# Cross attention of a Perceiver block: folds two at a time between the halves of the Wo and context products, and ScalarE's exponentials last in most steps

## The reference, cut to what matters

```
x = x + xattn(layernorm(x), ctx)     # the stage that is changed
x = x + attn(layernorm(x))
x = x + ffn(layernorm(x))            # shared expert and 2 of 8 routed experts

def xattn(query, ctx):               # query 64 x 64 x 256, ctx 64 x 256 x 256
    q = query @ Wq + bq              # 16 heads of 64
    k = ctx @ Wk + bk;  v = ctx @ Wv + bv
    attn = softmax(q k^T / 8)
    out = (attn v) @ Wo + bo + query
    return layernorm(out) * gamma + beta
```

## Time and profile before

| what | value |
|---|---|
| time, median of 3 runs | 2296.89 us (2295.93 to 2297.06) |
| the profiled execution's own time | 2297.97 us |
| its span | 2296.2 us |
| TensorE busy | 2151.3 us, 94% of the span |
| VectorE, ScalarE, GpSimd busy | 1584.7, 1267.9 and 709.7 us |
| a group of the cross attention | 88.46 us (603.64 to 692.10) |
| cross attention | to about 1440 us of the span |

### The profile page before, as it was taken

The page is one execution under the profiler, slowest core; times in us unless marked ns, Lnnn a source line. Parts: engine busy times, 40 slices in busy tenths (PEclk is TensorE's granted clock), DMA queues, the critical chain, the costliest instruction groups (busy, mean ns, idle before and its releaser), DMA issues. The chain is left out here.

```text
span 2296.2 us, 48591 instructions
## 1 busy us (share of the span) xinstructions
PE 2151.3 (94%) x16836; PEld 1870.7 (81%) x16837; DVE 1584.7 (69%) x2992; ACT 1267.9 (55%) x3071; POOL 709.7 (31%) x677
## 2 busy tenths in 40 slices
PE   6999999999999999999999999788897996999997
PEld 6888888888888888888888888667775885888886
DVE  6767767767768667677677676578885755666665
ACT  5656555555556556555565555356664334555554
POOL 4001001001011010010010010367774274777775
PEclk9999999999999999999999999899997998999999
DMA  4001001000010010010010001252224221333332
GB/s 145 15 15 33 14 18 32 6 26 23 9 32 23 9 32 18 14 32 18 14 32 14 18 10 40 85 182 76 78 76 163 82 86 39 54 53 54 55 53 44
DMA packets 103215, 104.41 MB, mean 45 GB/s; under 512 B 14064, under 2 KB 92656, under 8 KB 103152
## 3 DMA queue, kind: packets, MB, share of 16 engines
q1 hardware_dynamic: 87280, 84.62, 11.7%
q0 software_dynamic: 15872, 18.95, 5.2%
HBM read 72.73 MB, written 30.81 MB: 45 GB/s over the span
## 5 line engine op out<-in xcount | busy, mean ns | idle before, releaser
L534 ACT ACTIVATE probs<-banks,nbias 128x256 f32<-128x256 f32 x512 | 235.6, 474 | 231.7 <-DVE nbias L664 231.3
L876 PE MATMUL banks<-ctxT_hi,qk_hi 128*128 128x256 f32 x1024 | 302.0, 295 | 0.0
L876 PE MATMUL banks<-ctxT_hi,qk_lo 128*128 128x256 f32 x1024 | 290.4, 284 | 0.0
L876 PE MATMUL banks<-ctxT_lo,qk_hi 128*128 128x256 f32 x1024 | 289.3, 282 | 0.0
L622 DVE TENSOR_TENSOR pT_lo<-banks,pT_hi 128x512 fp32r<-128x512 f32 x256 | 166.4, 685 | 165.2 <-ACT pT_hi L496 163.8
L496 ACT ACTIVATE qk_hi<-banks 128x512 fp32r<-128x512 f32 x256 | 139.7, 619 | 153.7 <-PE banks L919 150.7
L622 DVE TENSOR_TENSOR qk_lo<-banks,qk_hi 128x512 fp32r<-128x512 f32 x256 | 158.8, 682 | 86.7 <-ACT qk_hi L496 86.7
L876 PE MATMUL banks<-pT_hi,ctx_hi 128*128 128x512 f32 x512 | 208.0, 406 | 3.9 <-DVE pT_lo L622 2.9
L422 POOL TENSOR_TENSOR rstd<-mv,power 128x2 f32<-128x2 f32 x32 | 22.2, 693 | 603.1 <-DVE mv L705 603.1
L876 PE MATMUL banks<-pT_hi,ctx_lo 128*128 128x512 f32 x512 | 202.1, 395 | 0.0
L876 PE MATMUL banks<-pT_lo,ctx_hi 128*128 128x512 f32 x512 | 200.9, 392 | 0.0
(11 more groups left out here) (258 smaller groups left out, 5955.8 us busy)
## 6 DMA issues: line engine op xcount, KB each, us to landing
ctx_raw<-in_ctx_dram SPq DMA_DIRECT2D x64, 256.0 KB, 2.7
experts_w<-in_L_ffn_We_dram SPq DMA_DIRECT2D x24, 512.0 KB, 8.3
x_in<-in_x_dram SPq DMA_DIRECT2D x16, 256.0 KB, 2.9
x_again<-in_x_dram SPq DMA_DIRECT2D x16, 256.0 KB, 2.8
x_stream<-z SPq DMA_DIRECT2D x16, 256.0 KB, 2.2
s_x<-x_stream SPq DMA_DIRECT2D x32, 128.0 KB, 2.1
s_x_again<-x_stream SPq DMA_DIRECT2D x32, 128.0 KB, 2.1
x_normalised<-s_xl SPq DMA_DIRECT2D x32, 128.0 KB, 1.7
```

Source lines behind the costliest of these rows:

```text
L534: nc.scalar.activation(probs[:, s % 2, p, :], scores[:, s % 2, p // 2, (p % 2) * SK:(p % 2 + 1) * SK], ACT.Exp, bias=nbias[:, s % 2, p:p + ...
L876: last = nc.tensor.matmul(out, a, b, start=(n == 0), stop=(n == 3 * len(pairs) - 1))
```

## The change

Three edits, all of order; no instruction of arithmetic is added or removed.

1. Steps 3 and 7 (`b == 3`): before, two folds (`EARLY = 2`), both halves of pc, six folds. Now a loop of four turns has two folds at the end of each turn, and ahead of them at most one piece of other work. In step 7: folds 0 and 1; pc 0, folds 2 and 3; pc 1, folds 4 and 5; qbk, folds 6 and 7. In step 3: o 0, folds 0 and 1; o 1, folds 2 and 3; pc 0, folds 4 and 5; pc 1, folds 6 and 7. The ring's order, TensorE, ScalarE and VectorE follow alike.
2. VectorE in step 7: the remainders of folds 0 and 1 come ahead of `peaks`.
3. ScalarE: the exponentials of steps 0, 1, 4, 5 and 7 come at the end of the step, behind the read-out of pc and pT, where they were ahead of them. Those of steps 2, 3 and 6 keep their place, but in step 3 they now stand ahead of folds 0 and 1.

```
+def part_of_pc(half, i):
+    c = i - (1 if half else 2)
+    return c if 0 <= c < DC else None
...
 # TensorE; ScalarE, VectorE and ring_order have the same loop
-                if s == 3 and g.prev:
-                    do_o(g)
-                if b == 3 and (g.next if half else g.cur):
-                    do_fold(g, half, range(EARLY))
-                if (g.cur if s >= 2 else g.prev):
+                if b == 3:
+                    for i in range(HALF // 2):
+                        c = part_of_pc(half, i)
+                        if s == 3 and g.prev and i < TILES:
+                            do_o(g, i)
+                        if g.cur and c is not None:
+                            do_pc(g, s, [c])
+                        if s == 7 and g.next and i == 3:
+                            do_qbk(g)
+                        if (g.next if half else g.cur):
+                            do_fold(g, half, (2 * i, 2 * i + 1))
+                elif (g.cur if s >= 2 else g.prev):
                     do_pc(g, s)
-                if b == 3 and (g.next if half else g.cur):
-                    do_fold(g, half, range(EARLY, HALF))
-                if s == 7 and g.next:
-                    do_qbk(g)
...
 # ScalarE
-                if b == 3 and (g.next if half else g.cur):
-                    for h in range(EARLY):
-                        fold_upper(g, half, h)
-                if g.cur:
+                if g.cur and s in (2, 3, 6):
                     exps(g, s)
...
                 if (g.cur if s >= 1 else g.prev):
                     for k in range(KC):
                         pT_upper(g, s, k)
+                if g.cur and s not in (2, 3, 6):
+                    exps(g, s)
...
 # VectorE
                 if s == STEPS - 1 and g.next:
                     ctx_lower(g, b)
+                    for h in range(2):
+                        fold_lower(g, half, h)
                 if g.cur:
                     peaks(g, s)
...
+                if b == 3:
+                    for i in range(half, HALF // 2):
+                        if s == 3 and g.prev and i < TILES:
+                            bank, free = wait_filled(dve, g, ("o", i))
+                            nc.vector.tensor_tensor(z[:, i, :], bank[:, 0:D], resid[:, i, :], ALU.add).then_inc(free, 1)
+                        if s == 7 and g.next and i == 3:
+                            keep_qbk(g)
+                        if (g.next if half else g.cur):
+                            for h in (2 * i, 2 * i + 1):
+                                fold_lower(g, half, h)
```

## The result

Measured together with the kernel before, 6 runs each: 2242.07 us (2240.76 to 2244.75) against 2295.7 us (2291.99 to 2297.06), a ratio of 0.9769 with a 95% interval of 0.9757 to 0.9782. The kernel is 53.6 us faster; 42.7 were predicted against the same median. The profiled execution took 2244.75 us, its span is 2243.0.

The account below looks back on a forecast made before the run. TensorE, busy 94%, was taken as the bound. Savings of 2.92 us a group, 41 over 14 groups, 43 with groups 0 and 15, plus 2 for the clock, gave 2253 us; range 2244 to 2264, wider 2238 to 2280.

Parts of the forecast that it names:

- my own case: Whole kernel at 2244 to 2264 us, smaller terms off by a third, step 7 by 0.5 us; chance 0.60.
- more than I count: Rival: all of step 7's 2.89 us saved, no loss in step 5; 2234 us, or 2243 with half; chance 0.08.
- Step 7: Fold pairs spread between pc and qbk: 13.15 us in place of 15.05, 1.90 saved, bounds 0 and 2.89.
- Step 3: Both halves of o spread between pairs of folds: 17.5 us, 0.5 saved, bounds 0 and 0.6.
- Steps 1, 2 and 6: With exponentials last, pT and q are read out sooner: 0.25, 0.25 and 0.29 us saved per group.
- Step 5: Later exponentials delay the context's remainder, whose bank pT awaits: 0.27 us lost, bounds 0 and 1.81.
- The clock: TensorE's lower-clock stretch in step 0 after step 7, 0.88 us in three groups, mostly goes: 2 us saved.
- Group 0: Full step 7 saving, but 1.1 us lost in step 3, where no o covers the exponentials; 0.8 saved.
- Group 15 and the rest: Last group saves 1.0 us in steps 1 to 3; no saving was counted outside the groups.
- no net change: Rival: step 5 loses its bound of 1.81 us, a third of step 7's gain is gone; chance 0.04.
- The slower rival: Late softmax exceeds TensorE's 5.71 us cover between pTs; at 0.8 us a step the kernel takes 2316; chance 0.07.
- the clock rival: Each hand-over idles TensorE and its clock dips in every group: 2264 to 2275 us; chance 0.05.

Follow-up runs that it names:

- mended kernel: Changed kernel, with VectorE taking the context's remainder ahead of the maximum in step 5 and group 0's step 3 exponentials last: 2229.47 us, 0.9704 of before.
- the doses: Changed kernel with two or four more exponentials into a spare tile, ahead of the four in steps 0, 1, 4, 5 and 7: 2263.65 and 2350.36 us.
- four extra exponentials: Changed kernel with four more exponentials into a spare tile, ahead of the four in steps 0, 1, 4, 5 and 7: 2350.36 us, 1.0241 of before.
- two extra exponentials: Changed kernel with two more exponentials into a spare tile, ahead of the four in steps 0, 1, 4, 5 and 7: 2263.65 us, 0.9863 of before.

## Why the prediction was right

The mechanism was right and the size too small: 45 us of the profiled execution's time were predicted, 53.2 came (2297.97 to 2244.75). The median of 2242.07 lies in the wide range, 2238 to 2280, but 2 us below the 2244 to 2264 of my own case. It is near the 2243 of the rival "more than I count", and that is a coincidence: the rival wanted all of step 7's 2.89 and no loss in step 5, and step 7 gave 1.96 while step 5 lost 0.33. The surplus comes from step 3, the clock, group 0 and what lies outside the loop, which all came out larger than I had them.

- **Step 7**, 1.90 predicted, 1.96 measured; the waits left are where the schedule had them, two of the five of a size that shows. The experiments add what the schedule could not: all three edits are needed for it. Edit 3 alone gives 1.39. Edits 1 and 3 without 2 give 0.75. Edits 1 and 2 without 3 give a longer step than before.
- **Step 3** is the term of the loop that was mis-sized most: 0.50 predicted, 0.77 measured, 3.8 us in 14 groups. By the distances between TensorE's starts, a tile of o takes 3.27 us where I had halved the 6.72 of before, and pT 0.79 and not 0.85. The kernel with edits 1 and 2 alone has all of the 0.77.
- **Steps 1, 2 and 6**: 0.25, 0.25 and 0.29 predicted, 0.25, 0.23 and 0.27 measured.
- **Step 5** lost 0.33 where I said 0.27, by the bank that I named: pT's wait for it went from 0.30 to 0.63. The mended kernel shows that it is this bank alone.
- **The loop in sum**: 3.15 a group and not 2.92, 44.1 and not 41.
- **The clock**: 2 us predicted. Groups 1 to 14 took 47.6 us less, 3.5 more than 14 times 3.15, and that is the lower clock of three groups, of which none is left. I had priced the 0.88 of step 0 alone; the stretch at the lower clock begins in the step 7 ahead of it, which took 15.78 us in place of 15.05:

```profile
542.25:558.03 15.78, 14.29 (x96) 12.46 (x94) 12.75 (x24) 8.98 (x22) 3.24 (x3) 0.95 0.23 66
```

- **Group 0** gained 2.2 and not 0.8, though its step 3 lost 4.0 (12.62 to 16.58) and not 1.1: I saw that no o covers its exponentials, but priced the wait at a third of its 3.25 us and left out the clock, 0.80 granted there and 0.87 before. What outweighed it are its steps 1 (8.69 to 7.43), 2 (15.57 to 13.27) and 7 (14.80 to 12.12), which I had taken like the loop's or not at all. A part of step 2's gain is the clock too (0.89 granted before, 0.99 after). That the sum of group 0 came out on the right side, with its largest term priced so wrongly, was luck.
- **Group 15 and the rest** gained 1.5 and 1.9, where I had 1.0 and nothing. The kernel after spreads by 4 us over six runs, so the 1.9 outside the changed groups can be chance.

Three pieces of its arithmetic don't hold. The softmax's 1.05, 1.81 and 1.45 add up to 4.31 and not 4.35, so the slack by hand is 1.40. The rival "no net change" at its own prices still leaves the kernel 8 to 12 us faster. And the range 2238 to 2280 leaves out the 2234 of "more than I count" too.

The slower rival, late exponentials as the bound, did not come, and the doses show how near it was: the slack is 1.28 us in step 0 and 1.44 in step 1. The four extra exponentials, a delay of 1.90, do make the kernel slower than before, as the rival said, though for the most part by another road: of the 6.9 us a group, 1.7 lie in steps 0 and 1 and 5.2 in steps 2, 5 and 6, where TensorE waits for `q_st` (up to 1.4 us) and `ctxT_lo` (2.4), which ScalarE and VectorE now read out late.

Of the clock rival, that the clock would dip in every group, the opposite happened: the changed kernel has more hand-overs in step 7, less idle time, and no group of the loop at a lower clock. The Trainium skill's "TensorE: Matmul & The Clock Gate", section "A second HAM failure mode: psum-queue depth-cycling", says that brief idling between groups of matmuls, as they cycle through PSUM banks, can cost the clock again and again. The kernel before fits that in part: three groups have a stretch at a lower clock, and no single wait in their step 7 is over 0.93 us. For the changed kernel, with more hand-overs but shorter waits, it does not hold, and the measurement decides. In the kernel with the folds' order alone, at 0.84 in a step 7, the waits are long, up to 2.69 us.

## What to carry to other kernels

Where one engine is saturated and the rest wait for a short ring of banks, the order of the ring alone can be worth something, here 1.96 of 15.05 us in step 7 with the same four banks: put work that is read out once, or takes long to compute, between the results that two engines must read out, and read out what frees a bank before what only feeds a later step. The two belong together: in step 7 the new order of the ring paid only once the engines that free the banks followed it. A chain with slack, here the softmax, can be pushed last on its engine; work out the slack from the trace as a sum to the instruction that needs it, and look for the one step where another chain already used it. Write such a steady loop down by hand, instruction by instruction, and treat the first pass through it apart, since its cover is not there.

## What the runs showed that was not expected

How the granted clock went with TensorE's idle time in a step (its length less its busy time) of a group in the loop; the last column counts all 15 groups that have the step:

| kernel, step | idle us | longest wait of a weight load | groups at a lower clock |
|---|---|---|---|
| changed, 7 | 0.05 | 0.48 | 0 |
| exponentials alone, 7 | 0.55 | 0.93 | 0 |
| two extra exponentials, 5 | 1.26 | 1.5 | 0 |
| edit 2 undone, 7 | 1.46 | 1.61 | 3 |
| before, 7 | 1.53 | 0.93 | 3 |
| four extra exponentials, 5 | 2.17 | 2.41 | 13 |
| folds' order alone, 7 | 2.8 | 2.69 | 15 |

With four extra exponentials step 6 has another 1.24 us idle, where the lower clock goes on. A group at the lower clock takes 0.4 to 3.4 us longer. The number of groups goes up with the idle time in the table, while the longest wait by itself does not order it: 0.93 stands both for none and for three. No kernel was made to change one of the two and keep the other, and what decides stays open.
